# Cross-attentions: the output product behind the first shares, the next rows normed ahead of the maxima, and the weighed values ahead of the scores two batches on

## The reference

```python
q = (x @ Wq.T + bq).reshape(B, N, H, D)
k = (context @ Wk.T + bk).reshape(B, M, H, D)
v = (context @ Wv.T + bv).reshape(B, M, H, D)
scores = jnp.einsum('bnhd,bmhd->bhnm', q, k) * SCALE
bias = jnp.where(ctx_key_padding_mask[:, None, None, :] != 0, 0.0, neg)
attn = jax.nn.softmax(scores + bias, axis=-1)
out = jnp.einsum('bhnm,bmhd->bnhd', attn, v).reshape(B, N, C)
return out @ Wo.T + bo          # the caller: x = x + xattn(layernorm(x), ctx)
```

## Time and profile before

| what | value |
|---|---|
| median of 3 runs | 3536.51 us (3529.74, 3536.51, 6857.02) |
| profiled execution, its own time | 3526.22 us |
| span of the profiled execution | 3524.3 us |
| granted TensorE clock, mean | 0.962 |
| busy: PE, PEld, DVE, ACT, POOL | 92%, 73%, 64%, 42%, 28% of the span |

### The profile page before, as it was taken

One profiled execution on the slowest core, in us unless ns is written; L12 is line 12 of the kernel. 1 busy time (PEld: TensorE's weight loads), 2 busy tenths in 40 slices (PEclk: granted clock), 3 DMA queues, 4 the chain that ended last, 5 costly groups with the idle time before them and its releaser, 6 DMA issues. The chain is left out here.

```text
span 3524.3 us, 105565 instructions
## 1 busy us (share of the span) xinstructions
PE 3238.8 (92%) x39150; PEld 2571.9 (73%) x39150; DVE 2251.4 (64%) x7505; ACT 1470.8 (42%) x4212; POOL 997.8 (28%) x1620
## 2 busy tenths in 40 slices
PE   8978999999887999999999999878999999988799
PEld 6767877777666888888877777765666777767576
DVE  4766326667667988889466666763334666668555
ACT  2334335555532333333255555541111555556222
POOL 0112113333243444444323333442110111112421
PEclk9999999999998999999999999979999999999799
DMA  6643331212112000000011111042112111110323
GB/s 230 211 179 152 106 105 55 57 54 57 58 55 88 2 2 2 2 2 2 17 40 48 43 43 41 2 161 85 46 44 72 39 38 39 39 35 2 112 80 113
DMA packets 145872, 225.26 MB, mean 64 GB/s; under 512 B 14216, under 2 KB 121480, under 8 KB 143816
## 3 DMA queue, kind: packets, MB, share of 16 engines
q1 hardware_dynamic: 138816, 203.16, 18.1%
q0 software_dynamic: 6816, 18.69, 1.4%
HBM read 201.03 MB, written 38.74 MB: 68 GB/s over the span
## 5 line engine op out<-in xcount | busy, mean ns | idle before, releaser
L3309 POOL TENSOR_TENSOR l1fu_second_weighed<-l1fu_second,l1fu_parts 128x256 bf16<-128x256 bf16 x384 | 272.6, 737 | 343.4 <-DVE l1fu_second L3550 336.5
L3361 PEld LDWEIGHTS l1fu_ps_u<-l1f_xnT_all,l1f_key_in 128*128 128x128 f32 x2048 | 252.6, 195 | 17.8 <-issue 11.6
L3361 PE MATMUL l1fu_ps_u<-l1f_xnT_all,l1f_key_in 128*128 (+1 forms) x2048 | 255.2, 279 | 9.1 <-issue 7.5
L3372 PE MATMUL l1fu_ps_y<-l1f_key_out,l1fu_units 128*128 128x256 f32 x1024 | 250.6, 389 | 1.6 <-DVE l1fu_units L3558 1.6
L3372 PEld LDWEIGHTS l1fu_ps_y<-l1f_key_out,l1fu_units 128*128 128x128 f32 x1024 | 185.7, 190 | 33.2 <-issue 6.2
L3423 ACT COPY l1fu_plane<-l1fu_ps_p 128x512 f32<-128x512 f32 x128 | 74.9, 585 | 249.8 <-PE l1fu_ps_p L3351 249.8
L3545 DVE TENSOR_TENSOR l1fu_first<-l1fu_index,l1fu_counted 128x1024 bf16<-128x1024 bf16 x128 | 164.7, 1287 | 20.8 <-PE l1fu_ps_p L3351 18.1
L3431 ACT ACTIVATE l1fu_units<-l1fu_ps_u 128x512 f32<-128x512 f32 x128 | 76.4, 597 | 150.9 <-PE l1fu_ps_y L3372 138.6
L1024 ACT ACTIVATE l2x_scores<-l2x_scores,l2x_minus_big 128x257 f32<-128x257 f32 x256 | 128.7, 509 | 12.7 <-DVE l2x_minus_big L1110 10.9
L1024 ACT ACTIVATE l1x_scores<-l1x_scores,l1x_minus_big 128x257 f32<-128x257 f32 x256 | 128.7, 510 | 12.3 <-DVE l1x_minus_big L1110 10.4
L1024 ACT ACTIVATE l3x_scores<-l3x_scores,l3x_minus_big 128x257 f32<-128x257 f32 x256 | 128.5, 505 | 11.4 <-DVE l3x_minus_big L1110 9.7
(11 more groups left out here) (747 smaller groups left out, 8435.9 us busy)
## 6 DMA issues: line engine op xcount, KB each, us to landing
rows_by_expert<-in_zeros_dram SPq DMA_DIRECT2D x1, 17544.0 KB
l0x_ctxT<-in_ctx_T_dram SPq DMA_DIRECT2D x32, 514.0 KB, 5.2
l0x_ctx_rows<-in_ctx_dram SPq DMA_DIRECT2D x64, 256.0 KB, 3.4
l0f_w<-in_L_ffn_w_dram SPq DMA_DIRECT2D x16, 1024.0 KB, 5.0
l1x_ctx_sb<-in_ctx_T_dram SPq DMA_DIRECT2D x64, 256.0 KB, 3.3
l2x_ctx_sb<-in_ctx_T_dram SPq DMA_DIRECT2D x64, 256.0 KB, 3.5
l3x_ctx_sb<-in_ctx_T_dram SPq DMA_DIRECT2D x64, 256.0 KB, 2.8
l1x_mask_raw<-in_mask_int_dram SPq DMA_DIRECT2D x16, 514.0 KB, 4.2
```

The costliest lines, as they stand in the source:

```text
L3309: last = nc.gpsimd.tensor_tensor(second_weighed[:, k % 2, part], second[:, k % 2], parts[:, 1 - par, part, TC * k:TC * k + TC].unsqueeze(2 ...
L3361: last = nc.tensor.matmul(ps_u[:, k % 2, j, :], key_in[:, c, JS * k + j, :], xnT_all[:, c, bass.ts(tile, P)], start=(c == 0), stop=(c == C ...
L3372: last = nc.tensor.matmul(ps_y, units[:, k, j, :], key_out[:, JS * k + j, :], start=(k + j == 0), stop=(k == K - 1 and j == JS - 1))
```

## The change

On GpSimd, x plus bo goes from the head of batch turn 0 to behind the shares. On TensorE, the output product of the tile before goes behind `turn_shares`, and the weighed values of `now` go ahead of the scores of `ahead2`. On VectorE, `add_output` goes behind `keep_probs`, and `tile_normed` goes from the end of batch turn 0 to right behind `add_output`. No instruction is added or removed.

```diff
@@ GpSimd, turn
-                    if t == 0:
-                        if "bo" in rows:
-                            after(pool, s["x_done"], n - 1)
-                            nc.gpsimd.tensor_tensor(x_plus_bo[:], core.x[:, i, :], rows["bo"][:], ALU.add).then_inc(
-                                s["x_biased"], 1)
-                        if not last:
-                            layer_norm_root(pool, nc, s, n + 1, mean[:], rstd[:], core.table("minus_half"))
+                    if not last and t == 0:
+                        layer_norm_root(pool, nc, s, n + 1, mean[:], rstd[:], core.table("minus_half"))
                     if not first and t == 0:
                         put_tail_values(i, n)
                     if ahead:
                         shares(ahead, before)
+                    if t == 0 and "bo" in rows:
+                        after(pool, s["x_done"], n - 1)
+                        nc.gpsimd.tensor_tensor(x_plus_bo[:], core.x[:, i, :], rows["bo"][:], ALU.add).then_inc(
+                            s["x_biased"], 1)
@@ TensorE, turn
                     if ahead3:
                         keys(ahead3, ahead)
-                    if not first and t == 0:
-                        tile_output(n - 1, n)
                     if not last and t == 1:
                         turn_xn(n + 1)
                     turn_probs_2(now, before, is_draining(t, last))
                     turn_shares(now, before)
+                    if not first and t == 0:
+                        tile_output(n - 1, n)
                     if ahead3:
                         values(ahead3, ahead2)
+                    outputs(now)
                     if ahead2:
                         score(ahead2, ahead, ahead3)
-                    outputs(now)
@@ VectorE, turn
-                    if not first and t == 0:
-                        add_output(i - 1, n - 1)
                     if not last and t == 2:
                         spread_q(n + 1)
                     keep_probs(now, before2, is_draining(t, last))
+                    if not first and t == 0:
+                        add_output(i - 1, n - 1)
+                    if not last and t == 0:
+                        tile_normed(i + 1, n + 1)
...
                     weigh(now, before)
-                    if not last and t == 0:
-                        tile_normed(i + 1, n + 1)
```

## The result

The changed kernel takes 3546.11 us (median of 13, 3539.76 to 3557.81), the kernel before 3529.74 us (median of 13). The ratio is **1.0049**, 95% interval [1.0036, 1.0062]: slower by half a per cent. Forecast were 3505 us, a little faster, and a range up to 3545. The profiled execution took 3546.11 us against 3526.22 before, 19.9 us more. One run of the kernel before was disturbed (6857.02 us) and is left out of the ratio.

What follows compares the result with a forecast made beforehand. TensorE was taken as the bound, busy 420 of 443 us in cross-attention. Gains of 62.6 us less 33 for stalls and 4 for drains gave -25.6, 3501 from the profiled execution; forecast 3505 us, range 3469 to 3545.

Steps and rivals of the forecast that it cites:

- The output product and the norm: TensorE's waits for oT and the normed rows vanish: 0.39 and 1.00 us gained, 45 times, 62.6 us.
- Weighed values ahead of the scores: Keys stall 0.29 us (0.11 to 0.45) for the first maximum to free the score bank, 135 times; 33 us lost.
- The first maximum's start: On VectorE, 0.80 us after S, the scores' start, the middle between S + 0.69 and S + 0.90.
- The handover: From the first maximum's end to TensorE resuming with the keys: 0.07 us taken, from 0 to 0.13.
- What a stall costs: Delay of the keys' weight load past its unhindered start, S + 1.01 (S: scores' start); 0.29 us forecast.
- My sign of being wrong: The keys' new wait on VectorE's first maximum being above 0.43 us or absent; about 0.3 us was expected.
- The drain: In each stage's last tile, scores come later without keys or values as cover: 1.3 us × 3, 4 us lost.
- The loop's end: A third of the keys' stalls, where transposes start later after the work before them: 0.13 us smaller, 0.16 each.
- the term of 0 for the pairings of array shapes: Changed neighbours among TensorE's values, weighed values, scores and transposes cost 0, give or take 7 us.
- B: Rival: score bank comes so late at the keys' wait that the kernel is slower, +37, 3567 us; chance 0.14.
- A: Rival: score bank is read in time, stalls shrink to 10 us, drain costs nothing; 3477 us; chance 0.20.
- C: Rival: no change, through VectorE slipping or array shapes costing 7 us with stalls at their upper end; 3533 us; chance 0.16.

Runs made afterwards that it cites:

- e1: Changed kernel with only the order of the weighed values undone, scores first again; 3462.96 us, ratio 0.9826 to the kernel before.
- e8: Changed kernel with the old order of scores and weighed values in the last tile alone; 3534.76 us, ratio 1.0012 to the kernel before.
- f1: The probe: changed kernel with a one-column copy from the last score bank replacing the no-operation ahead of the maxima; 3542.48 us, ratio 1.0050.
- e7: Kernel before with the score bank given back by the second maximum instead of the first, 0.35 us later; 3542.79 us, ratio 1.0035.
- e2: Kernel before with only the weighed values put ahead of the scores; 3611.99 us, ratio 1.0241.

## Why the prediction was wrong

**The output product and the norm** were forecast at 62.6 us. e1, which has both and no swap, is 0.0174 × 3530 = 61 us faster (its tiles are 1.49, 1.42 and 1.43 us shorter in the three stages). The places, the cover on VectorE (the norm at 728.37 to 728.78, the values' copy at 729.31) and GpSimd's part were right. The product's own spacing also fell from 0.97 to 0.87, which I had not priced.

**The step that failed** is "Weighed values ahead of the scores". Its mechanism, place and count were right: the keys wait for the first maximum, 45 times a stage, not in batch turn 2. Its size was wrong, 0.29 us where 0.58 was measured, and it lies outside the 0.11 to 0.45 that I allowed. *The first maximum's start* is the term: I took S + 0.80 and called its upper end S + 0.90; it is S + 1.03 in l1x and most of l2x, and S + 1.00 in l3x. I had a row that said 1.03 and explained it away by the copy ahead of it. The last tile's rows held the check: scores at 950.02, the next maximum at 951.05 behind quite other work of VectorE, again 1.03. The l1x prologue's 0.90 was the exception, and I let it bound the rule. It is one of three such places a stage, all in the first tile, at 0.89 to 0.91 (l2x's very first is 1.26). The changed kernel has them too, with VectorE idle:

```profile
538.45 0.69 PE L869 MATMUL l1x_ps_s<-l1x_kT,l1x_q_by_half 32*64 32x257 f32 x16
...
539.34 0.43 DVE L1102 CUSTOM_DVE_ANT_0 l1x_scores<-l1x_ps_s,l1x_bias 128x257 f32<-128x257 f32 x1 [0.68 <-PE l1x_ps_s L869]
```

In the code of the maxima what differs there is that their two waits on the tile before are left out. Whether these 0.14 us are theirs was not tested. *The handover* is the smaller term: 0.12 us (723.91 to 724.03) where I took 0.07, inside its 0 to 0.13. Put in, the sum closes: 1.03 + 0.43 + 0.12 - 1.01 = 0.57. *What a stall costs* was priced rightly, by the weight load's delay: the load starts at S + 1.59 instead of S + 1.01, and the 0.58 shows in the keys as 0.50 in their start and 0.08 behind it. My sign of being wrong, a wait above 0.43 us, would have missed this, as the wait on the row is 0.34. *The drain*: 4 us forecast, 9.3 measured by the products' starts and 11.5 by e8, as the lower clock and the wait chain of the last batch were not in the term. The loop's end was right: 0.13 less there. So was the term of 0 for the pairings of array shapes: the starts are still 0.58 and 0.62 us apart (729.20 to 729.78, 729.78 to 730.40 in the changed kernel).

With 0.58 and 11.5 the sum would have read 90 × 0.58 + 45 × 0.45 + 11.5 - 62.6 = +21 us; measured +19.9 between the profiled executions. The l1x stage, forecast 8 to 9 us shorter, is 5.4 longer from its first matmul to its last output product. From the ratios of the changed kernel and e1, the swap cost 0.0223 × 3530 = 79 us inside the change, where I had 37.

**The rivals.** B, the slower one, came true by its own place and rule: it decides from a mean stall of 0.43 us, and the mean stall is 0.54. Its price of +37, taken from the l2x row, was too high (+19.9 measured), but its sign was right; I gave it 0.14. A fell, as no stall shrank. C, +3 us, came near in size only: neither VectorE's slip nor the array shapes cost anything. The Trainium skill, TensorE: Matmul & The Clock Gate, "The cost: per-tile semaphore tail", gave an estimate of 89 ns, which the prediction set behind the modelled end, so that the maxima would begin near S + 0.89. The first tiles show 0.89 to 0.91, all others 1.00 or more, and the probe has 0.21 us between that end and VectorE's start, VectorE's own start included. So the estimate lay on the right side of my middle and was still too small: a stall of 0.38 by it, 0.58 measured. The Trainium skill says in Perfetto Trace Analysis, "Tensor Engine Instruction (MATMUL, LD_WEIGHTS)", that a matmul's shown end is estimated and the semaphore's way comes after it; the probe agrees.

Still open: in l2x each tile loses 0.11 us more than in l1x, with the first maximum of batch turn 0 at S + 1.13 (1981.34 to 1982.47). It vanished with the probe (27.16 in all three stages), but I didn't find what holds it.

## What to carry to other kernels

Measure a chain start to start, in every place where it occurs, ahead of any bound from modelled ends. If one distance stays the same (here 1.03 us from scores to maximum in all of l1x behind its first tile, in the kernel before) while the work ahead of the waiting engine differs, the distance is the chain, and an engine that merely becomes free at that moment hides it. A place where the distance is shorter (here the first tile) is not a bound until you know what the program does differently there. Before moving work from behind a producer to ahead of it, ask which wait that work was covering: these 0.58 us of weighed values were the cover of the score bank's return, and they pay only where other work (here the queries) stands in for them. A stall added ahead of an older wait on the same queue can be free (e7), unless it also makes the awaited engine later (e2), so stalls don't add up by count.

## What the runs showed of the hardware

- From a group of sixteen tiled matmuls to a dependent VectorE copy it took 0.21 us beyond the modelled end (f1), and to the maximum behind a no-operation 0.34 us; in a stage's first tile the latter was 0.20.
- Sixteen of the thirty-two weighed-value matmuls, set between other array shapes, took 0.36 us where all thirty-two together take 0.58.
- The drains of 20 us in which TensorE waited 1.63 and 1.40 us (l1x) and 1.63 and 1.41 (l2x) ran at a granted clock of 0.65, the one with 1.60 and 0.90 (l3x) at 0.91. With the old order (1.05 and 0.79 in l1x) they ran at 0.90 to 1.00.
- A keys call that had to wait ran 1.80 us to the next start instead of 1.72, as its first weight load no longer lay under the transposes.
